# Switched attention: pair matrices on two turned tiles at once, in every second slot, with the routing and rounding steps moved

## The chip, the cores and the metric

One core of one Trainium2 chip. The metric is the device time of one execution of the whole program in microseconds (us). TensorE is called PE, VectorE DVE, ScalarE ACT, GpSimd POOL and SyncE, which issues the DMAs, SP.

## What is computed

A block of four gated layers on x, 128 x 64 x 128 float32, with cross attention and feed forward parts. The change touches only the last part, a switched attention with 8 heads and 8 experts:

```python
logits = jnp.einsum('bsd,ed->bse', x, w)           # w: sel_v_w or sel_o_w
probs = jax.nn.sigmoid(logits.reshape(B, S, H, E))
vals, idx = jax.lax.top_k(probs, K)                # K = 2
vals = vals / jnp.clip(vals.sum(-1, keepdims=True), 1e-09) * route_scale
gate = (jax.nn.one_hot(idx, E) * vals[..., None]).sum(-2)
```

With x normalised per row, q = x q_w, k = x k_w (head size 128), v is the sum over the 8 experts of gate_v times x v_w, the softmax of q k / sqrt(128) over 64 positions multiplies v, and the output is the sum over heads and experts of gate_o times that context times o_w, scaled by a gate and added to the residual. The scores of a head are x (q_w k_w) x, so one 128 x 128 matrix a head, the pair matrix, takes the place of two projections.

## The kernel before

The rows are cut into 64 tiles of 128 (two sequences of 64 positions each). `program` (L2347) runs an opening, a chain of the first layers, and then `switch_attention` (L1731), which is some 60% of the time. There each engine has a list of stages (lag, step), and `straight` (L36) writes the engine's stream out: in slot t every stage in the list's order, each for tile t - lag. Each engine works its stream off in that order; semaphores join the engines. So the work's order is the order of five lists written by hand.

In a slot PE has eight v units, `unit("v", h)`, for the tile of lag 2 and eight o units, `unit("o", h)`, for the tile of lag 3. A unit (L2202 and on) is six matmuls with 512 moving columns in rounded float32 (`F32R`), three each into the banks ps_a and ps_d: high by high, high by low, low by high. `xT_high` is the turned tile rounded, `xT_low` what rounding leaves. ACT's `scale` (L1947) takes ps_a into one of four buffers `scaled`, by the gate, in four activations a unit; DVE's `mix` (L2092) takes ps_d. POOL's `add_v` (L1884) adds both to v (two additions a head), `add_o` does the same for the output, and `finish` (L1922) closes an output tile with three additions. A unit waits for its banks (freed by the unit two before it); ACT's scaling waits for POOL's addition of the unit four before it.

Between the units stand the smaller steps. In PE's list: `turn_x` (L2225) turns the normalised tile into ps_m; `turn_probs` turns the softmax, four heads at a time; `logits` multiplies the turned tile with the routing weights; `pair_keys(0)` and `pair_keys(1)` (L2245) multiply four pair matrices each with one turned tile, into the banks ps_w0 and ps_w1; `scores` (L2271) multiplies the turned tile with uT, what came of the pair matrices; `context` (L2259) multiplies the turned softmax with v, into the same two banks ps_w. A float32 matmul appears as two instructions.

ACT's list has `keep_x` (L1966) after v1: two activations out of ps_m, to xT and to xT_high; `exp_logits` and `keep_probs` after v3; `keep_u(0)` after v5 and `keep_u(1)` after v6 (ps_w to uT); `keep_ctx` and the exponentials among the o units. POOL's list is:

```python
stages = [(2, add_v(0)), (2, add_v(1)), (1, low_x), (4, finish)] + [(2, add_v(h)) for h in range(2, SH)]
stages += [(3, add_o(h)) for h in range(6)] + [(0, rstd)] + [(3, add_o(h)) for h in range(6, SH)]
```

`low_x` (L1877) waits for xT_high of its tile. DVE's list has the mixes and, between them, the 20 routing operations (`route`, L2121), the row maximum, `low_ctx`, the moments of the next tile, and in slots 2 and 3 the splitting of the 16 halves of the o weights (`low_o`, L2060); ACT rounds these halves in the same slots (`round_o`), and SP's list brings them (`fetch_o`, L1859) through four buffers.

Of the kernel before, what the change touches and what calls it, by code (L numbers as in the profile page):

```python
# [1730 lines left out]
def switch_attention(k, A, C, x_in, out):  # L1731
# [6 lines left out]
    with k.scope():  # L1738
# [31 lines left out]
        place = k.sb("sw_place", [P, 2 * SH, SE])  # L1770
# [3 lines left out]
        r = {n: k.sb("sw_r_" + n, G) for n in ("plus", "p", "eq1", "w1", "sel1", "p2", "eq2", "w2", "sel2", "sel")}  # L1774
# [47 lines left out]

        with nc.Block() as block:
            @block.sync
            def _(sp):
# [5 lines left out]
                sp.dma_start(place[:], A["c_place"].rearrange("p (g e) -> p g e", e=SE)).then_inc(q["place"], 16)  # L1831
# [35 lines left out]
                straight([(0, fetch), (1, only_first(fetch_v)), (1, only_first(fetch_o(0, 4))), (2, fetch_residual),  # L1867
                          (2, only_first(fetch_o(4, 10))), (3, only_first(fetch_o(10, 16))), (4, store)])
# [4 lines left out]
            def _(pool):  # L1873
# [65 lines left out]
                stages = [(2, add_v(0)), (2, add_v(1)), (1, low_x), (4, finish)] + [(2, add_v(h)) for h in range(2, SH)]  # L1939
                stages += [(3, add_o(h)) for h in range(6)] + [(0, rstd)] + [(3, add_o(h)) for h in range(6, SH)]  # L1940
# [3 lines left out]
            def _(act):  # L1944
# [90 lines left out]
            def _(dve):  # L2035
# [85 lines left out]
                def route(n):  # L2121


                    def step(i, s, rd):
                        ops = [
                            lambda: dve.tensor_scalar(r["plus"][:], decays[:], 1.0, None, ALU.add),
                            lambda: dve.reciprocal(r["p"][:], r["plus"][:]),
                            lambda: dve.tensor_reduce(rm["m1"][:], r["p"][:], AX.X, ALU.max),
                            lambda: dve.tensor_tensor(r["eq1"][:], r["p"][:], wide(rm["m1"][:]), ALU.is_equal),
                            lambda: dve.tensor_tensor(r["w1"][:], r["eq1"][:], place[:], ALU.mult),  # L2130
                            lambda: dve.tensor_reduce(rm["w1"][:], r["w1"][:], AX.X, ALU.max),
                            lambda: dve.tensor_tensor(r["sel1"][:], r["w1"][:], wide(rm["w1"][:]), ALU.is_equal),
                            lambda: dve.scalar_tensor_tensor(out=r["p2"][:], in0=r["sel1"][:], scalar=-2.0, in1=r["p"][:],
                                                             op0=ALU.mult, op1=ALU.add),
                            lambda: dve.tensor_reduce(rm["m2"][:], r["p2"][:], AX.X, ALU.max),
                            lambda: dve.tensor_tensor(r["eq2"][:], r["p2"][:], wide(rm["m2"][:]), ALU.is_equal),
                            lambda: dve.tensor_tensor(r["w2"][:], r["eq2"][:], place[:], ALU.mult),
                            lambda: dve.tensor_reduce(rm["w2"][:], r["w2"][:], AX.X, ALU.max),
                            lambda: dve.tensor_tensor(r["sel2"][:], r["w2"][:], wide(rm["w2"][:]), ALU.is_equal),
                            lambda: dve.tensor_tensor(r["sel"][:], r["sel1"][:], r["sel2"][:], ALU.add),  # L2140
                            lambda: dve.tensor_tensor(chosen[:, s], r["p"][:], r["sel"][:], ALU.mult),
# [245 lines left out]
```

## Time and profile before

| | before |
|---|---|
| three runs, us | 3166.52, 3166.97, 3173.21 (median 3166.97) |
| the profiled execution, us | 3168.74 |
| its span, first to last instruction, us | 3167.0 |
| busy in the span, us | PE 2907.0, DVE 2780.7, ACT 2341.8, POOL 2322.8 |
| granted TensorE clock, mean | 0.941 of full speed |
| DMA, mean | 17 GB/s |

The span holds all layers. The profiled execution has its own time, 1.8 us above the median of the three runs, and a duration read from the trace belongs to it. Busy is the time in which an engine has an instruction; matmuls overlap, so for PE the start of one to the start of the next is the better measure. An idle time in brackets stands in front of the instruction that ended it, with what released it.

### The profile page before, as it was taken

What the parts mean: (1) busy time and instruction counts of PE and PEld (TensorE: products, weight loads), DVE (VectorE), ACT (ScalarE), POOL (GpSimd) and SP (SyncE); (2) the same over time, 40 slices, a digit from 0 to 9 for tenths busy, and PEclk for the clock granted to TensorE, in tenths of its full rate; (3) what the DMA queues carried; (4) which work ended last, traced back from release to release, by engine and by line L of the source; (5) the groups of instructions that cost most, each with busy time, mean ns of one, the idle gap of its engine ahead of it and who ended that gap; (6) DMA issues with size and microseconds to landing.
All of it is one profiled execution on the core that took longest, in us unless ns stands there. A gap on an engine that the chain in (4) does not pass through costs nothing.

```text
span 3167.0 us, 78218 instructions
## 1 busy us (share of the span) xinstructions
PE 2907.0 (92%) x24620; PEld 2176.0 (69%) x24620; DVE 2780.7 (88%) x9085; ACT 2341.8 (74%) x7546; POOL 2322.8 (73%) x3112
## 2 busy tenths in 40 slices
PE   7489992897689996999999999999999999999998
PEld 7257762675357774677777777777777777777776
DVE  6789997899989986888888888898898898898897
ACT  4866668888976665777777777777777777777776
POOL 2799994666876662677777777777777777777777
PEclk8589995898789997999999999999999999999999
DMA  4000000220000004100000000000000000000000
GB/s 131 8 2 2 2 2 18 68 75 13 1 6 16 16 16 109 30 9 8 7 9 8 7 9 8 7 9 8 7 9 8 8 9 8 7 9 8 7 8 6
DMA packets 114508, 55.31 MB, mean 17 GB/s; under 512 B 18352, under 2 KB 113712, under 8 KB 114096
## 3 DMA queue, kind: packets, MB, share of 16 engines
q1 hardware_dynamic: 114096, 50.30, 5.8%
q8 instruction: 200, 3.28, 0.4%
q14 instruction: 212, 1.74, 0.2%
HBM read 41.81 MB, written 8.45 MB: 16 GB/s over the span
## 4 chain that ended last, share of the span: by engine, by line
PE 59%; DVE 1%; ACT 1%; POOL 1%; DMA 0%; issue 0%; SPq 0%; POOLq 0%; ACTq 0%; DVEq 0%
PE ps_sw_a L2221 24%; PE ps_sw_d L2221 22%; PE ps_sw_w L2267 4%; PE ps_sw_w L2254 3%; PE ps_sw_s L2236 2%; PE ps_sw_s L2278 2%; PE ps_sw_m L2243 1%; ACT sw_scaled L1962 0%; DVE sw_v_part L2117 0%; PE ps_sw_m L2229 0%; DMA sw_v<-in_L_ffn_v_w 0%; POOL sw_v_pair L1889 0%; DVE sw_v_low L2056 0%; DVE sw_o_low L2063 0%; ACT sw_v_high L2017 0%
## 5 line engine op out<-in xcount | busy, mean ns | idle before, releaser
L1962 ACT ACTIVATE sw_scaled<-ps_sw_a,sw_gate_o 128x128 f32<-128x128 f32 x2048 | 620.3, 447 | 254.1 <-PE ps_sw_a L2221 247.0
L1962 ACT ACTIVATE sw_scaled<-ps_sw_a,sw_gate_v 128x128 f32<-128x128 f32 x2048 | 597.3, 448 | 196.2 <-PE ps_sw_a L2221 194.4
L2117 DVE SCALAR_TENSOR_TENSOR sw_o_part<-ps_sw_d,sw_gate_o,sw_o_part 128x128 f32<-128x128 f32 x1920 | 555.6, 339 | 63.1 <-PE ps_sw_d L2221 60.5
L1889 POOL TENSOR_TENSOR sw_v_pair<-sw_v_part,sw_scaled 128x256 f32<-128x256 f32 x512 | 381.9, 746 | 157.0 <-DVE sw_v_part L2117 91.6
L2117 DVE SCALAR_TENSOR_TENSOR sw_v_part<-ps_sw_d,sw_gate_v,sw_scaled 128x128 f32<-128x128 f32 x1024 | 303.9, 337 | 126.1 <-PE ps_sw_d L2221 107.1
L1915 POOL TENSOR_TENSOR sw_o_rest<-sw_o_rest,sw_scaled 128x256 f32<-128x256 f32 x384 | 285.4, 743 | 158.0 <-ACT sw_scaled L1962 120.7
L2117 DVE SCALAR_TENSOR_TENSOR sw_v_part<-ps_sw_d,sw_gate_v,sw_v_part 128x128 f32<-128x128 f32 x1024 | 304.8, 339 | 0.0
L1918 POOL TENSOR_TENSOR sw_o_rest<-sw_o_rest,sw_scaled 128x256 f32<-128x256 f32 x384 | 282.6, 736 | 30.1
L1894 POOL TENSOR_TENSOR sw_v<-sw_v_pair 128x128 f32<-128x128 f32 x512 | 244.6, 478 | 40.1
L1014 POOL TENSOR_TENSOR at_key_wide<-at_keyT,c_half_heads 128x1024 f32<-128x1024 f32 x128 | 242.6, 1895 | 4.6 <-ACT at_keyT L1112 4.6
L2221 PE MATMUL ps_sw_a<-sw_v_high,sw_xT_high 128*128 128x512 f32 x512 | 234.5, 458 | 8.2 <-DVE sw_v_low L2056 8.2
L2221 PE MATMUL ps_sw_a<-sw_o_high,sw_ctx_high 128*128 128x512 f32 x512 | 215.7, 421 | 0.2 <-ACT sw_scaled L1962 0.2
L2221 PE MATMUL ps_sw_d<-sw_v_high,sw_xT_high 128*128 128x512 f32 x512 | 207.6, 405 | 0.3 <-DVE sw_v_part L2117 0.3
L2221 PE MATMUL ps_sw_d<-sw_o_high,sw_ctx_high 128*128 128x512 f32 x512 | 202.1, 395 | 1.2 <-DVE sw_v_part L2117 1.2
L2221 PE MATMUL ps_sw_d<-sw_o_low,sw_ctx_high 128*128 128x512 f32 x512 | 202.7, 396 | 0.0
L2221 PE MATMUL ps_sw_a<-sw_o_high,sw_ctx_low 128*128 128x512 f32 x512 | 202.7, 396 | 0.0
L2221 PE MATMUL ps_sw_a<-sw_v_high,sw_xT_low 128*128 128x512 f32 x512 | 202.5, 396 | 0.0
L2221 PE MATMUL ps_sw_a<-sw_v_low,sw_xT_high 128*128 128x512 f32 x512 | 202.2, 395 | 0.0
L2221 PE MATMUL ps_sw_d<-sw_o_high,sw_ctx_low 128*128 128x512 f32 x512 | 202.1, 395 | 0.0
L2221 PE MATMUL ps_sw_a<-sw_o_low,sw_ctx_high 128*128 128x512 f32 x512 | 202.1, 395 | 0.0
L2221 PE MATMUL ps_sw_d<-sw_v_high,sw_xT_low 128*128 128x512 f32 x512 | 201.8, 394 | 0.0
L2221 PE MATMUL ps_sw_d<-sw_v_low,sw_xT_high 128*128 128x512 f32 x512 | 200.7, 392 | 0.0
(337 smaller groups left out, 8511.3 us busy)
## 6 DMA issues: line engine op xcount, KB each, us to landing
re_values<-in_ctx SPq DMA_DIRECT2D x128, 64.0 KB, 2.4
l_ctx<-in_ctx SPq DMA_DIRECT2D x16, 256.0 KB, 4.5
x<-in_x SPq DMA_DIRECT2D x16, 256.0 KB, 4.6
re_ctx<-in_ctx SPq DMA_DIRECT2D x16, 256.0 KB, 3.1
scratch_x<-x SPq DMA_DIRECT2D x64, 64.0 KB, 1.5
sw_x<-scratch_x SPq DMA_DIRECT2D x64, 64.0 KB, 1.9
sw_x_res<-scratch_x SPq DMA_DIRECT2D x64, 64.0 KB, 1.8
out<-sw_y SPq DMA_DIRECT2D x64, 64.0 KB, 1.5
```

What stands on the lines that cost most here:

```text
L1014: pool.tensor_tensor(key_wide[:, s], keyT[:, s].unsqueeze(1).broadcast_to([P, HALF, P]), C["half_heads"][:].unsqueeze(2).broadcast_to([P, ...
L1889: pool.tensor_tensor(v_pair[:, h % 2], v_part[:, h], scaled[:, h % 4, 2:4], ALU.add)\
L1894: pool.tensor_tensor(v[:, h], v_pair[:, h % 2, 0], v_pair[:, h % 2, 1], ALU.add).then_inc(q["v"], 1)
L1915: pool.tensor_tensor(o_rest[:, 0:2], o_rest[:, 0:2], scaled[:, h % 4, 0:2], ALU.add)\
L1918: pool.tensor_tensor(o_rest[:, 2:4], o_rest[:, 2:4], scaled[:, h % 4, 2:4], ALU.add)\
L1962: act.activation(scaled[:, h % 4, e], ps_a[h % 2][:, e], ACT.Copy, scale=gates[:, s, h, HALF_E + e:HALF_E + e + 1]).then_inc(a_scaled[kind ...
L2117: dve.scalar_tensor_tensor(out=acc[:, e % 2], in0=ps_d[h % 2][:, e], scalar=gates[:, s, h, e:e + 1], in1=before, op0=ALU.mult, op1=ALU.add ...
L2221: m = pe.matmul(bank, lhs[a], w[b][:, h, experts], start=c == 0, stop=c == 2)
L2236: m = pe.matmul(ps_s[t, h], probs[t, s, h], C["ident"][t, t], start=True, stop=True)
L2254: m = pe.matmul(ps_w[n][:, h * P:(h + 1) * P], W["pair"][:, 4 * n + h], xT[:, s], start=True, stop=True)
L2267: m = pe.matmul(ps_w[b][:, h * S:(h + 1) * S], v[t, h], probs_T[t, h], start=True, stop=True)
L2278: m = pe.matmul(ps_s[t], xT[:, s, t], uT[:, :, t], start=True, stop=True)
```

## The change

The lags of nearly everything behind the turning of a tile grow by two: logits, routing, scores and exponentials from 1 to 3, v units from 2 to 4, o units from 3 to 5, finish from 4 to 6. xT has four buffers instead of two and uT holds two tiles. The pair matrices are multiplied for an even tile and the one after it at once, so with 256 moving columns, in every second slot: two groups of 4 matmuls, one behind the first four turned heads of the softmax, one behind v4. keep_x keeps xT alone; the rounding to xT_high is the new step round_x, of lag 3. The routing's ten buffers become three, written in place, and place is one row broadcast. The splitting of the o weights keeps its lags, 2 and 3.

```diff
-        xT = k.sb("sw_xT", [P, 2, P])
+        xT = k.sb("sw_xT", [P, 4, P])
-        uT = k.sb("sw_uT", [P, SH, P])
+        uT = k.sb("sw_uT", [P, SH, 2, P])
...
-        place = k.sb("sw_place", [P, 2 * SH, SE])
+        place = k.sb("sw_place", [P, SE])
-        r = {n: k.sb("sw_r_" + n, G) for n in ("plus", "p", "eq1", "w1", "sel1", "p2", "eq2", "w2", "sel2", "sel")}
+        r = {n: k.sb("sw_r_" + n, G) for n in ("equal", "sel", "p2")}
...
+        def of_pair(step):
+            def at(i, s, rd):
+                if i % 2 == 0:
+                    step(i, s, rd)
+            return at
...
-                straight([(0, fetch), (1, only_first(fetch_v)), (1, only_first(fetch_o(0, 4))), (2, fetch_residual),
-                          (2, only_first(fetch_o(4, 10))), (3, only_first(fetch_o(10, 16))), (4, store)])
+                straight([(0, fetch), (1, only_first(fetch_v)), (1, only_first(fetch_o(0, 4))), (4, fetch_residual),
+                          (2, only_first(fetch_o(4, 10))), (3, only_first(fetch_o(10, 16))), (6, store)])
...
-                stages = [(2, add_v(0)), (2, add_v(1)), (1, low_x), (4, finish)] + [(2, add_v(h)) for h in range(2, SH)]
-                stages += [(3, add_o(h)) for h in range(6)] + [(0, rstd)] + [(3, add_o(h)) for h in range(6, SH)]
+                stages = [(4, add_v(0)), (4, add_v(1)), (3, low_x), (6, finish)] + [(4, add_v(h)) for h in range(2, SH)]
+                stages += [(5, add_o(h)) for h in range(6)] + [(0, rstd)] + [(5, add_o(h)) for h in range(6, SH)]
...
                 def keep_x(i, s, rd):
                     act.wait_ge(q["x_turned"], i + 1)
+                    if not first(i, 4):
+                        act.wait_ge(q["scores"], i - 3)
+                        act.wait_ge(q["xT_low"], i - 3)
+                    act.activation(xT[:, i % 4], ps_m[:, 0], ACT.Copy).then_inc(q["xT"], 1)
+
+                def round_x(i, s, rd):
+                    act.wait_ge(q["xT"], i + 1)
                     if not first(i, 2):
-                        act.wait_ge(q["scores"], i - 1)
                         act.wait_ge(q["xT_low"], i - 1)
                         act.wait_ge(d_made["v"], SH * (i - 1))
-                    act.activation(xT[:, s], ps_m[:, 0], ACT.Copy).then_inc(q["xT"], 1)
-                    act.activation(xT_high[:, s], ps_m[:, 0], ACT.Copy).then_inc(q["xT_high"], 1)
+                    act.activation(xT_high[:, s], xT[:, i % 4], ACT.Copy).then_inc(q["xT_high"], 1)
...
-                stages = vs[:2] + [(1, keep_x)] + vs[2:4] + [(1, exp_logits), (2, keep_probs)] + vs[4:6]
-                stages += [(1, keep_u(0)), vs[6], (1, keep_u(1)), vs[7]] + os[:3] + [(2, keep_ctx(0)), os[3], exps[0]]
-                stages += [os[4], (2, keep_ctx(1)), os[5], exps[1], os[6], exps[2], os[7], exps[3]]
+                stages = vs[:2] + [(1, keep_x), vs[2], (3, keep_u(0)), vs[3], (3, keep_u(1)), (3, exp_logits), (4, keep_probs)]
+                stages += [vs[4], (3, round_x), vs[5], (3, keep_u(2)), vs[6], (3, keep_u(3)), vs[7]] + os[:3]
+                stages += [(4, keep_ctx(0)), os[3], exps[0], os[4], (4, keep_ctx(1)), os[5], exps[1], os[6], exps[2], os[7], exps[3]]
...
-                def pair_keys(n):
+                def pair_keys(lo):
                     def step(i, s, rd):
...
+                        if lo == 0:
+                            pe.wait_ge(q["xT"], i + 2)
+                        for n in (lo, lo + 1):
+                            if n >= 2:
+                                pe.wait_ge(q["uT"], 2 * i + n - 1)
+                            elif i == 0:
+                                pe.wait_ge(prep["kept"], 3)
+                            else:
+                                pe.wait_ge(q["ctx_low"], 2 * (i - 2) + n + 1)
+                            both = xT[:, i % 4:i % 4 + 2].rearrange("p c t -> p (c t)")
+                            for h in range(2):
+                                m = pe.matmul(ps_w[n % 2][:, 2 * h * P:2 * (h + 1) * P], W["pair"][:, 2 * n + h], both,
+                                              start=True, stop=True)
+                            m.then_inc(q["u"], 1)
+                    return of_pair(step)
...
-                stages = vs[:2] + [(1, turn_x), turns[0], vs[2], turns[1], (1, logits), vs[3], vs[4], (1, pair_keys(0))]
-                stages += [vs[5], (1, pair_keys(1)), vs[6], vs[7], os[0], (1, scores), os[1], (2, context)]
-                stages += os[2:]
+                stages = vs[:2] + [(1, turn_x), turns[0], (3, pair_keys(0)), vs[2], turns[1], (3, logits), vs[3], vs[4], (3, pair_keys(2))]
+                stages += vs[5:] + [os[0], (3, scores), os[1], (4, context)] + os[2:]
```

ACT's keep_u has four parts now (0 to 3) that run in the same slots as the pair groups, each after the unit named in the list. DVE's list keeps its order with the new lags.

## Rows read from the trace of the kernel before

**Rows 1.** Windows of two neighbouring slots: busy us and instructions of each engine.
```profile
2406.70:2436.30 29.60, 29.60 (x184) 22.68 (x184) 26.56 (x96) 22.55 (x91) 22.64 (x36) 1.00 0.03 9
2436.30:2465.90 29.60, 29.60 (x184) 22.69 (x183) 26.59 (x96) 22.54 (x91) 22.64 (x36) 1.00 0.03 8
```

**Rows 2.** Timeline of PE in one slot: start, duration, line, operation, count.
```profile
2406.72 0.47 PE L2221 MATMUL ps_sw_a<-sw_v_high,sw_xT_high 128*128 128x512 f32 x1
...
2410.56 0.50 PE L2221 MATMUL ps_sw_a<-sw_v_high,sw_xT_high 128*128 128x512 f32 x1
...
2413.00 0.47 PE L2221 MATMUL ps_sw_a<-sw_v_high,sw_xT_high 128*128 128x512 f32 x1
...
2414.47 0.39 PE L2221 MATMUL ps_sw_a<-sw_v_high,sw_xT_high 128*128 128x512 f32 x1
...
2415.61 0.39 PE L2221 MATMUL ps_sw_d<-sw_v_high,sw_xT_low 128*128 128x512 f32 x1
2415.83 1.05 PE L2254 MATMUL ps_sw_w<-sw_xT,sw_pair 128*128 128x128 f32 x8
2416.64 0.48 PE L2221 MATMUL ps_sw_a<-sw_v_high,sw_xT_high 128*128 128x512 f32 x1
2416.95 0.40 PE L2221 MATMUL ps_sw_a<-sw_v_low,sw_xT_high 128*128 128x512 f32 x1
...
2425.50 0.40 PE L2221 MATMUL ps_sw_d<-sw_o_high,sw_ctx_low 128*128 128x512 f32 x1
2425.83 2.00 PE L2267 MATMUL ps_sw_w<-sw_probs_T,sw_v 64*128 64x64 f32 x32
```

**Rows 3.** Timeline of ACT in the same slot.
```profile
2410.42 0.61 ACT L1972 ACTIVATE sw_xT<-ps_sw_m 128x128 f32<-128x128 f32 x1
2410.57 0.61 ACT L1973 ACTIVATE sw_xT_high<-ps_sw_m 128x128 fp32r<-128x128 f32 x1
...
2413.97 1.14 ACT L1962 ACTIVATE sw_scaled<-ps_sw_a,sw_gate_v 128x128 f32<-128x128 f32 x4 [1.27 <-PE ps_sw_a L2221]
...
2415.62 1.18 ACT L1962 ACTIVATE sw_scaled<-ps_sw_a,sw_gate_v 128x128 f32<-128x128 f32 x4
...
2419.89 1.14 ACT L1962 ACTIVATE sw_scaled<-ps_sw_a,sw_gate_v 128x128 f32<-128x128 f32 x4 [0.64 <-PE ps_sw_a L2221]
2420.90 0.61 ACT L1993 ACTIVATE sw_uT<-ps_sw_w 128x512 f32<-128x512 f32 x1
2421.38 1.16 ACT L1962 ACTIVATE sw_scaled<-ps_sw_a,sw_gate_v 128x128 f32<-128x128 f32 x4
```

**Rows 4.** Timeline of POOL in the same slot.
```profile
2413.31 0.46 POOL L1881 TENSOR_TENSOR sw_xT_low<-sw_xT,sw_xT_high 128x128 fp32r<-128x128 f32 x1
2413.73 0.73 POOL L1925 TENSOR_TENSOR sw_o_pair<-sw_o_rest 128x256 f32<-128x256 f32 x1
...
2415.82 0.72 POOL L1889 TENSOR_TENSOR sw_v_pair<-sw_v_part,sw_scaled 128x256 f32<-128x256 f32 x1
...
2417.04 0.74 POOL L1889 TENSOR_TENSOR sw_v_pair<-sw_v_part,sw_scaled 128x256 f32<-128x256 f32 x1
...
2419.86 0.74 POOL L1889 TENSOR_TENSOR sw_v_pair<-sw_v_part,sw_scaled 128x256 f32<-128x256 f32 x1 [0.27 <-DVE sw_v_part L2117]
...
2422.13 0.74 POOL L1889 TENSOR_TENSOR sw_v_pair<-sw_v_part,sw_scaled 128x256 f32<-128x256 f32 x1 [1.00 <-ACT sw_scaled L1962]
...
2424.40 0.74 POOL L1889 TENSOR_TENSOR sw_v_pair<-sw_v_part,sw_scaled 128x256 f32<-128x256 f32 x1 [1.00 <-DVE sw_v_part L2117]
2425.22 0.46 POOL L1894 TENSOR_TENSOR sw_v<-sw_v_pair 128x128 f32<-128x128 f32 x1
```

**Rows 5.** Timeline of ACT, then of DVE, at the stage's beginning.
```profile
1225.77 0.27 ACT L1973 ACTIVATE sw_xT_high<-ps_sw_m 128x128 fp32r<-128x128 f32 x1
...
1250.67 0.61 DVE L2117 SCALAR_TENSOR_TENSOR sw_v_part<-ps_sw_d,sw_gate_v,sw_scaled 128x128 f32<-128x128 f32 x2 [0.64 <-issue]
...
1251.71 0.68 DVE L2063 TENSOR_TENSOR sw_o_low<-sw_o_part,sw_o_high 128x512 fp32r<-128x512 f32 x1
...
1270.18 0.68 DVE L2063 TENSOR_TENSOR sw_o_low<-sw_spare,sw_o_high 128x512 fp32r<-128x512 f32 x1
...
1279.99 0.61 DVE L2117 SCALAR_TENSOR_TENSOR sw_v_part<-ps_sw_d,sw_gate_v,sw_scaled 128x128 f32<-128x128 f32 x2 [1.11 <-ACT sw_scaled L1962]
```

More of the change, by code:

```diff
@@ L1830, in _ @@
                 sp.dma_start(route_scale[:], on_all(A["L3_ffn_route_scale"], 1)).then_inc(prep["small"], 16)
[L1831 removed]
+                sp.dma_start(place[:], A["c_place"][:, 0:SE]).then_inc(q["place"], 16)
                 def tile_in(dst, i):
@@ L1880, in low_x @@
                         pool.wait_ge(d_made["v"], SH * (i - 1))
-                    pool.tensor_tensor(xT_low[:, s], xT[:, s], xT_high[:, s].bitcast(F32), ALU.subtract)\
+                    pool.tensor_tensor(xT_low[:, s], xT[:, i % 4], xT_high[:, s].bitcast(F32), ALU.subtract)\
                         .then_inc(q["xT_low"], 1)
@@ L1990, in step @@
                         act.wait_ge(q["u"], 2 * i + n + 1)
-                        if n == 0 and not first(i, 1):
+                        if n == 0 and i:
                             act.wait_ge(q["scores"], i)
-                        act.activation(uT[:, 4 * n:4 * n + 4], ps_w[n].rearrange("p (h t) -> p h t", h=4), ACT.Copy)\
-                            .then_inc(q["uT"], 1)
-                    return step
+                        act.activation(uT[:, 2 * n:2 * n + 2], ps_w[n % 2].rearrange("p (h c t) -> p h c t", h=2, c=2),
+                                       ACT.Copy).then_inc(q["uT"], 1)
+                    return of_pair(step)
                 def keep_ctx(b):
@@ L2124, in step @@
                     def step(i, s, rd):
+                        p = decays
                         ops = [
[L2126 to L2130, printed above, removed]
@@ new lines, in step @@
+                            lambda: dve.tensor_tensor(r["equal"][:], p[:], wide(rm["m1"][:]), ALU.is_equal),
+                            lambda: dve.tensor_tensor(r["equal"][:], r["equal"][:], place[:].unsqueeze(1).broadcast_to(G), ALU.mult),
+                            lambda: dve.tensor_reduce(rm["w1"][:], r["equal"][:], AX.X, ALU.max),
+                            lambda: dve.tensor_tensor(r["sel"][:], r["equal"][:], wide(rm["w1"][:]), ALU.is_equal),
+                            lambda: dve.scalar_tensor_tensor(out=r["p2"][:], in0=r["sel"][:], scalar=-2.0, in1=p[:],
@@ L2140, in step @@
-                            lambda: dve.tensor_tensor(r["sel"][:], r["sel1"][:], r["sel2"][:], ALU.add),
-                            lambda: dve.tensor_tensor(chosen[:, s], r["p"][:], r["sel"][:], ALU.mult),
+                            lambda: dve.tensor_tensor(r["equal"][:], r["p2"][:], wide(rm["m2"][:]), ALU.is_equal),
+                            lambda: dve.tensor_tensor(r["equal"][:], r["equal"][:], place[:].unsqueeze(1).broadcast_to(G), ALU.mult),
+                            lambda: dve.tensor_reduce(rm["w2"][:], r["equal"][:], AX.X, ALU.max),
@@ L2226, in turn_x @@
                     pe.wait_ge(q["xhat"], i + 1)
-                    if not first(i, 1):
-                        pe.wait_ge(q["decays"], i)
+                    if i >= 1:
+                        pe.wait_ge(q["xT"], i)
+                    if i >= 3:
+                        pe.wait_ge(q["decays"], i - 2)
                     pe.transpose(ps_m[:, 0], L["xhat"][:, s], C["ident"][:]).then_inc(q["x_turned"], 1)
@@ L2241, in logits @@
                         pe.wait_ge(prep["kept"], 1)
-                    pe.wait_ge(q["xT_high"], i + 1)
-                    pe.matmul(ps_m[:, 1], xT[:, s], W["sel"][:], start=True, stop=True).then_inc(q["logits"], 1)
-                def pair_keys(n):
+                    pe.wait_ge(q["xT"], min(i + 3, TILES))
+                    pe.matmul(ps_m[:, 1], xT[:, i % 4], W["sel"][:], start=True, stop=True).then_inc(q["logits"], 1)
+                def pair_keys(lo):
                     def step(i, s, rd):
-                        if i == 0:
-                            pe.wait_ge(prep["kept"], 2 + n)
-                        elif not first(i, 2):
-                            pe.wait_ge(q["ctx_low"], 2 * (i - 2) + n + 1)
-                        else:
-                            pe.wait_ge(q["uT"], 1 + n)
-                        for h in range(4):
-                            m = pe.matmul(ps_w[n][:, h * P:(h + 1) * P], W["pair"][:, 4 * n + h], xT[:, s],
-                                          start=True, stop=True)
-                        m.then_inc(q["u"], 1)
-                    return step
+                        if lo == 0:
[12 more added lines that the diff above has]
+                            m.then_inc(q["u"], 1)
+                    return of_pair(step)
@@ L2271, in scores @@
                 def scores(i, s, rd):
-                    waits = [(q["uT"], 2 * i + 2)]
+                    waits = [(q["uT"], 4 * (i // 2) + 4)]
                     if not first(i, 1):
@@ L2277, in scores @@
                         t = slice(b * S, (b + 1) * S)
-                        m = pe.matmul(ps_s[t], xT[:, s, t], uT[:, :, t], start=True, stop=True)
+                        m = pe.matmul(ps_s[t], xT[:, i % 4, t], uT[:, :, s, t], start=True, stop=True)
                     m.then_inc(q["scores"], 1)
```

42 lines of the change are left out of this document (22 added, 20 removed).

## The prediction

> **What bounds the kernel now.** I read the page's busy shares first, then the windows of two neighbouring slots of the switched stage, then one such slot engine by engine in the timeline. A slot is one turn of the order written out in the code: eight v units, eight o units, and everything placed between them. In the two windows PE is busy 29.60 of 29.60 us at full clock, DVE 26.56, POOL 22.64 and ACT 22.55 [rows 1]; 64 tiles at 29.6 us are 1894 of the 3167 us. So PE sets the time there, and the question is whether anything makes it wait. All offsets below count from the first v matmul of the slot, 2406.72 [rows 2].
>
> PE's order in a slot: v2 begins at 3.84, v3 at 6.28, v4 at 7.75, a pair group of 8 instructions at 9.11, and the context at 19.11. The last o matmul before the context begins at 2425.50; at the plain pitch of 0.23 (five in 1.14, 2414.47 to 2415.61) the context could begin at 2425.73, and it begins at 2425.83 [rows 2]. What it waits for is POOL's eighth v, 2425.22 + 0.46 = 2425.68 [rows 4], plus a handover of 0.15. **The context has only 0.1 us of slack against POOL.** POOL itself, between the xT_low subtraction at 6.59 and that last v, stands idle 0.27, 1.00 and 1.00, together 2.27 us [rows 4]. ACT is late only at the slot's start: it rounds xT_high at 3.85, scales v3 at 7.25 after 1.27 us of idleness, and v4 at 8.90 [rows 3]. POOL takes xT_low with no wait, because xT_high has lain ready for 2.5 us.
>
> **The change, part by part.** (1) The pair matmuls. Now a tile has two groups of 8 instructions of 128 columns. From the matmul before a group to the second one after it takes 2415.61 to 2416.95, 1.34 us, against 0.46 for two plain pitches: a group costs 0.89 [rows 2], four of them, two tiles, 3.56. Afterwards two tiles have 16 instructions of 256 columns, all in the odd slot. 0.89 over 8 is 0.111 for 128 columns, or 0.107 without the joints; at 0.2133 for 256 columns the 16 cost 3.41, with two joints of 0.04 left 3.49. That saves 0.07 per two tiles, 2 us in the run. The bounds: nothing at all, and 1.78 per two tiles if an instruction of 256 columns cost no more than one of 128, 57 us. The first is nearer: columns rule PE's rows, since 512 single-pass columns take 0.23 there. The Trainium skill ("TensorE: Matmul & The Clock Gate", Back-to-back issue gap) gives a sustained 81 ns a matmul at 128 columns and 131 at 512, which would put it near the second bound; the pitch of 0.23 at 512 columns here contradicts it.
>
> (2) Placement. In odd slots pair(0), 8 x 0.2133 = 1.71 us, stands ahead of v2; pair(2), 1.71 again, after v4. In even slots both are gone, and PE could be at the context 1.78 us sooner.
>
> (3) The rounding. This is the costly one. keep_x was one step with both activations, at 3.70 and 3.85. Now only xT is kept there, and round_x, which makes xT_high, stands in ACT's order **behind the scaling of v4**, at the same lag (3) as POOL's low_x. So POOL's wait on xT_high becomes a wait within the slot, and low_x is still POOL's third step: behind it are queued finish (three additions) and add_v(2) to add_v(7), on which the context hangs, and ACT's scaling too, whose buffers come free by these additions.
> Even slot: ACT's v4 begins at 8.90, four scalings take 1.01 (2419.89 to 2420.90) [rows 3], so round_x begins at 9.91; 0.27 for it alone [rows 5] and 0.15 handover put low_x at 10.3 instead of 6.59, 3.7 later. From there POOL goes without a gap: 0.42, 2.09 for finish, six additions of v at 1.23 (2415.82 to 2417.04) [rows 4]. Of the 3.7 its old idleness takes up 2.27 and the context's slack 0.1: **the context comes 1.3 later**. The 1.78 that PE gains on the way is lost in that wait.
> Odd slot: pair(0) puts v2, v3 and v4 on PE off by 1.71. keep_u(0) fits into ACT's old idleness of 1.27 before v3, but keep_u(1), 0.48 (2420.90 to 2421.38) [rows 3], stands between v3 and v4. ACT's v4 is 2.2 later, and low_x 3.7 + 2.2 = 5.9. Less 2.37: **the context comes 3.5 later**, of which pair(0) and pair(2) alone would have asked 1.6 beyond the old slot. After the context each slot goes on as now (ACT, DVE and POOL all wait for PE there), so a shift of the context is a longer slot.
> Sixty-one slots have low_x, finish and the v units together (6 to 66), 31 even and 30 odd: 31 x 1.3 + 30 x 3.5 = 145 us; slot 5, without finish, some 2.
>
> (4) Two more slots of lead. v units start in slot 4 instead of 2, but the splitting of the o weights stays in slots 2 and 3. DVE now does the first split at 1251.71 between the first mixes, and mixes tile 1 from 1279.99; the last split of slot 2 is at 1270.18 [rows 5]. Afterwards all 16 splits stand ahead of the first mix. Without mixes between them they are paced by their DMAs and by rounding; I estimate 20 to 25 us for both slots, so tile 0's mixes begin near 1272 instead of 1250.67. Given back: the slots that follow have no splits, 16 x 0.6, and the next tiles' softmax is ready. I take +9, between 0 and +20. The last slots are as now.
>
> (5) At nothing: ten routing buffers become three and place is broadcast, but the 20 operations are the same, and DVE has 3.0 us idle in a slot [rows 1]; without that cover each 0.1 us more per operation would be 2 us a tile. In odd slots the first routing step waits some 0.8 for the later exp, and DVE is shifted with PE. The residual load and the store are moved by two slots on SP's queue with their readers; the place load shrinks outside the loop.
>
> Sum: 145 + 2 + 9 = 156 us. Against the profiled execution (3167.0 span, 3168.74 in all) it is 3325; the three runs' median, 3166.97, lies 1.8 below, so I say 3323.
>
> **Rivals.** *A smaller loss* (0.07): POOL's chain gives way somewhere, or 256 columns are cheap, so that pair(0) shifts ACT's v4 by 0.85 less: 25 us off, and with half of the even slots' loss 45 off. 3210 to 3280. *A larger one* (0.03): scaling of v6 and v7 waits for the late add_v(2) and add_v(3), PE's units o0 and o1 for their banks, and this goes on past the context; one more us a slot gives 3385. *The change does nothing* (0.05): the wait on xT_high is hidden, and 2 us of saving stand against 9 of lead: 3174, from 3160 to 3185. It would need xT_high in 2.37 us after the old low_x, before 8.96, while ACT begins v4 only at 8.90 and round_x stands behind it. *Faster* (0.03): the same hidden wait and 256 columns at the price of 128, 0.89 a tile: 3167 - 57 + 9 = 3119. It decides once the rounding is visible before 8.96 and the wide group takes under 1.2 us instead of 1.71. The first speaks against the code's order, the second against the 0.23 of a 512-column matmul. By the page's two figures the time would be near this rival's, and its 0.03 is what these rows leave of it.
>
> **How the numbers follow.** The likeliest case (0.82) spans 3285 to 3365: 0.3 us either way on the shifts is 20, the lead another 10. To hold 8 in 10 and take in part of the smaller loss the range is 3255 to 3365. About 0.2% (6 us) is what a measurement here can tell from none. Faster: 0.03 and a little of the hidden case, 0.04. Same: 0.03. Slower: 0.93.
>
> **What would show it.** PE no longer full in the switched stage, with waits for POOL's v before the context of about 1.3 us in odd and 1.4 in even slots; POOL idle about 3.7 (even) and 5.9 (odd) before low_x, released by ACT's rounding; contexts alternating by about 31 and 33 us instead of 29.6; the wide group at 1.71 for 8 instructions; ACT waiting for POOL before scaling v6 in even slots, and o0 on PE some 1.5 us behind it. I am wrong if POOL waits little before low_x, if the context follows its o unit at 0.33, or if the slot keeps 29.6. If slots are as forecast but the end is not, the lead was mis-sized.

## The result, and the profile after

| | before | after |
|---|---|---|
| median beside each other on one chip, us | 3167.64 (4 runs) | 3359.66 (4 runs) |
| lowest and highest, us | 3166.52 to 3173.21 | 3349.52 to 3364.54 |
| the profiled execution, us | 3168.74 | 3358.62 |
| its span, us | 3167.0 | 3356.8 |
| granted TensorE clock, mean | 0.941 | 0.937 |

The changed kernel is slower: ratio 1.0598, 95% interval 1.0571 to 1.0626. The forecast was 3323 (3255 to 3365); between the two profiled executions the change costs 189.9 us, where the sum said 156.

The page of the changed kernel: span and busy times, the chain that ended last, and one of the costly groups (busy and mean ns, then the idle time before it and who ended it).

```profile
span 3356.8 us, 77191 instructions
...
PE 2972.7 (89%) x24108; PEld 2160.3 (64%) x24108; DVE 2797.1 (83%) x9085; ACT 2352.1 (70%) x7546; POOL 2322.8 (69%) x3112
...
POOL 26%; PE 19%; issue 12%; ACT 3%; DVE 3%; POOLq 0%; DMA 0%; SPq 0%; ACTq 0%; DVEq 0%
...
L1887 POOL TENSOR_TENSOR sw_xT_low<-sw_xT,sw_xT_high 128x128 fp32r<-128x128 f32 x64 | 29.6, 462 | 315.2 <-ACT sw_xT_high L1984 315.2
```

POOL's 64 subtractions for xT_low last 30 us together, and POOL stands 315 us idle in front of them, all of it for ACT's rounding. The chain that ended last now runs through POOL more than through PE.

Windows from one context to the next, an even slot and then an odd one (busy us and instructions of PE, PEld, DVE, ACT, POOL, then the granted clock):

```profile
2422.60:2453.66 31.06, 28.97 (x167) 20.59 (x167) 26.52 (x96) 21.73 (x86) 22.73 (x36) 1.00 0.03 8
2453.66:2487.06 33.40, 31.77 (x183) 23.76 (x184) 27.23 (x96) 23.63 (x90) 22.71 (x36) 1.00 0.03 7
```

In [rows 1] PE was busy for all of 29.60; here it misses 2.1 and 1.6 us a slot, at full clock. Some waits between 1400 and 3200 us (us in total, times, longest):

```profile
POOL sw_xT_low L1887 <- ACT sw_xT_high L1984: 274.8, 56, 6.1
...
ACT sw_scaled L1968 <- POOL sw_v_pair L1895: 127.5, 111, 2.6
...
PE ps_sw_w L2288 <- POOL sw_v L1900: 59.6, 55, 1.3
PE ps_sw_a L2233 <- ACT sw_scaled L1968: 37.1, 56, 1.2
```

PE's timeline: the o0 of the even slot, the two contexts that enclose the odd one (their counterpart is the last line of [rows 2]), and between them both wide groups:

```profile
2448.15 0.47 PE L2233 MATMUL ps_sw_a<-sw_o_high,sw_ctx_high 128*128 128x512 f32 x1 [0.98 <-ACT sw_scaled L1968]
...
2453.66 2.00 PE L2288 MATMUL ps_sw_w<-sw_probs_T,sw_v 64*128 64x64 f32 x32 [0.91 <-POOL sw_v L1900]
...
2468.03 1.99 PE L2272 MATMUL ps_sw_w<-sw_xT,sw_pair 128*128 128x256 f32 x8
2469.67 0.58 PE L2233 MATMUL ps_sw_a<-sw_v_high,sw_xT_high 128*128 128x512 f32 x1
...
2474.80 0.39 PE L2233 MATMUL ps_sw_d<-sw_v_high,sw_xT_low 128*128 128x512 f32 x1
2475.03 1.89 PE L2272 MATMUL ps_sw_w<-sw_xT,sw_pair 128*128 128x256 f32 x8
2476.56 0.58 PE L2233 MATMUL ps_sw_a<-sw_v_high,sw_xT_high 128*128 128x512 f32 x1
2476.98 0.40 PE L2233 MATMUL ps_sw_a<-sw_v_low,sw_xT_high 128*128 128x512 f32 x1
...
2487.06 2.00 PE L2288 MATMUL ps_sw_w<-sw_probs_T,sw_v 64*128 64x64 f32 x32 [1.25 <-POOL sw_v L1900]
```

ACT's timeline, the scaling of v6 and v7 in the even slot:

```profile
2446.81 2.36 ACT L1968 ACTIVATE sw_scaled<-ps_sw_a,sw_gate_v 128x128 f32<-128x128 f32 x8 [2.33 <-POOL sw_v_pair L1895]
```

POOL's timeline (compare [rows 4]), with the subtraction in an even and in an odd slot:

```profile
2443.51 0.46 POOL L1887 TENSOR_TENSOR sw_xT_low<-sw_xT,sw_xT_high 128x128 fp32r<-128x128 f32 x1 [3.75 <-ACT sw_xT_high L1984]
2443.93 0.74 POOL L1931 TENSOR_TENSOR sw_o_pair<-sw_o_rest 128x256 f32<-128x256 f32 x1
...
2453.16 0.45 POOL L1900 TENSOR_TENSOR sw_v<-sw_v_pair 128x128 f32<-128x128 f32 x1
...
2476.76 0.46 POOL L1887 TENSOR_TENSOR sw_xT_low<-sw_xT,sw_xT_high 128x128 fp32r<-128x128 f32 x1 [6.11 <-ACT sw_xT_high L1984]
```

From 2443.51 to 2453.16 POOL has no bracket: it works without a gap from the late rounding to v's last addition, and the context starts right behind that. Gone are the three idle times of [rows 4].

**Where the 189.8 us of span went.** The starts of the 64 contexts divide the stage. The first is at 1287.76 instead of 1272.22, 15.5 later; the last at 3323.39 instead of 3133.60, and behind it both kernels take 33.4. So the slots between cost 174.3. Against the usual 29.61, thirty odd slots are 33.40 long (114 us more), twenty even ones 31.04 (29 us), ten even ones 32.44 (28 us), one 34.19 (4.6 us); the mean before was a little over the usual one, which takes 1 us off this sum. The eleven long even slots owe their extra length to PE's clock, which the last section shows.

### The profile page after: what moved, and what is told of

Its sections match the earlier page's. It is cut to its first block, busy times and chain, and to the rows that moved or that the text cites. A ratio compares the mean times of both kernels' runs of the same rounds, so it can differ in the third digit from the quotient of the medians.

```text
span 3356.8 us, 77191 instructions
## 1 busy us (share of the span) xinstructions
PE 2972.7 (89%) x24108; PEld 2160.3 (64%) x24108; DVE 2797.1 (83%) x9085; ACT 2352.1 (70%) x7546; POOL 2322.8 (69%) x3112
## 4 chain that ended last, share of the span: by engine, by line
POOL 26%; PE 19%; issue 12%; ACT 3%; DVE 3%; POOLq 0%; DMA 0%; SPq 0%; ACTq 0%; DVEq 0%
PE ps_sw_a L2233 7%; POOL sw_v_pair L1895 7%; POOL sw_o_rest L1921 6%; POOL sw_o_rest L1924 6%; PE ps_sw_d L2233 5%; POOL sw_v L1900 4%; PE ps_sw_w L2288 4%; ACT sw_scaled L1968 3%; DVE sw_v_part L2128 1%; POOL sw_o_pair L1933 1%; POOL sw_o_pair L1931 1%; PE ps_sw_w L2272 1%; PE ps_sw_s L2299 1%; POOL sw_y L1937 1%; POOL sw_xT_low L1887 1%
## 5 line engine op out<-in xcount | busy, mean ns | idle before, releaser
L2233 PE MATMUL ps_sw_a<-sw_o_high,sw_ctx_high 128*128 128x512 f32 x512 | 224.4, 438 | 40.9 <-ACT sw_scaled L1968 40.9
L1887 POOL TENSOR_TENSOR sw_xT_low<-sw_xT,sw_xT_high 128x128 fp32r<-128x128 f32 x64 | 29.6, 462 | 315.2 <-ACT sw_xT_high L1984 315.2
L2233 PE MATMUL ps_sw_d<-sw_o_high,sw_ctx_high 128*128 128x512 f32 x512 | 211.7, 414 | 5.4 <-DVE sw_v_part L2128 5.3
```

What stands on the lines that cost most here:

```text
L1887: pool.tensor_tensor(xT_low[:, s], xT[:, i % 4], xT_high[:, s].bitcast(F32), ALU.subtract)\
L2233: m = pe.matmul(bank, lhs[a], w[b][:, h, experts], start=c == 0, stop=c == 2)
```

## The experiments

The kernels ran on several chips, whose medians of the kernel before lie between 3166.22 and 3173.60. So the table gives each kernel's ratio to the kernel before on the same chip (95% interval), and what one trace says of the contexts (the slots are the usual ones of the middle of the stage). A difference of a few us between traces of two chips can be the chips'. Four kernels, e7, e9, e10 and e12, leave out most of the routing; they only show what DVE's work costs.

| kernel | median, us | ratio, 95% interval | first context | odd, even slot |
|---|---|---|---|---|
| changed kernel | 3359.66 | 1.0571 to 1.0626 | 1287.76 | 33.40, 31.04 |
| e1 rounding early | 3257.35 | 1.0245 to 1.0280 | 1287.89 | 32.18, 29.55 |
| e2 before, rounding late | 3274.05 | 1.0306 to 1.0336 | 1271.52 | 31.06, 31.06 |
| e3 xT_low late on POOL | 3250.04 | 1.0234 to 1.0264 | 1283.20 | 32.18, 29.44 |
| e4 splits with the v units | 3354.26 | 1.0557 to 1.0589 | 1273.15 | 33.39, 31.04 |
| e5 e1 without the pairing | 3175.22 | 1.0017 to 1.0036 | 1283.82 | 29.63, 29.63 |
| e6 e1 and e4 | 3250.75 | 1.0244 to 1.0287 | 1273.83 | 32.17, 29.55 |
| e7 e1, some routing short | 3228.96 | 1.0178 to 1.0223 | 1280.35 | 31.79, 29.24 |
| e8 e1, 128 columns | 3251.19 | 1.0253 to 1.0287 | 1286.04 | 32.20, 29.53 |
| e9 e1, routing bare | 3180.28 | 1.0016 to 1.0034 | 1282.08 | 31.28, 28.15 |
| e10 before, routing bare | 3163.65 | 0.9967 to 0.9985 | 1269.70 | 29.64, 29.64 |
| e11 e5 and e4 | 3171.34 | 0.9997 to 1.0014 | 1273.88 | 29.63, 29.63 |
| e12 changed, routing bare | 3333.69 | 1.0500 to 1.0558 | 1281.14 | 33.10, 30.86 |

### e1: the rounding back behind keep_x

```diff
-stages = vs[:2] + [(1, keep_x), vs[2], (3, keep_u(0)), ...
+stages = vs[:2] + [(1, keep_x), (3, round_x), vs[2], (3, keep_u(0)), ...
-stages += [vs[4], (3, round_x), vs[5], ...
+stages += [vs[4], vs[5], ...
```

> The changed kernel with round_x moved directly behind keep_x, where the rounding stood before; all else as changed. Theory 1 (POOL's wait before low_x is the loss): the wait is gone, the odd slot is bound by PE at 29.60 + 1.64 = 31.2 us, the even slot at 27.9, and with the lead of 15.5 read from the changed kernel's first context the time is 3167 + 15.5 - 2 = 3180, within 8. Rival (the wide groups' place ahead of v2 holds up ACT and DVE by itself): the odd slots stay over 32.5 and the time is 3200 to 3290. Rival (lags and buffers): nothing changes, 3357.

Measured 3257.35, 84 above before and not the 3180 of the theory. The time is in the first rival's band, but the odd slots are not over its 32.5; the span is 100 below the changed kernel's. The waits on xT_high are gone from the trace, yet a slot is still 1.26 longer than before on average (32.18 and 29.55). The late rounding is about half of the loss; the other half I had not seen.

### e2: the late rounding alone, in the kernel before

```diff
-                    act.activation(xT_high[:, s], ps_m[:, 0], ACT.Copy).then_inc(q["xT_high"], 1)
+                def round_x(i, s, rd):
+                    act.wait_ge(q["xT"], i + 1)
+                    act.activation(xT_high[:, s], xT[:, s], ACT.Copy).then_inc(q["xT_high"], 1)
...
-[(1, exp_logits), (2, keep_probs)] + vs[4:6]
+[(1, exp_logits), (2, keep_probs), vs[4], (1, round_x), vs[5]]
...
-pe.wait_ge(q["xT_high"], i + 1)
+pe.wait_ge(q["xT"], i + 1)
```

(The last pair is the wait of `logits`, which reads xT and need not wait for the rounding.)

> The kernel before with one part of the change: the rounding is a step of its own behind the scaling of v4, at the old lag, and reads xT. Theory 1: POOL stands idle 3.7 us before low_x in every slot and the context comes 1.4 us later, 31.0 instead of 29.60: 3167 + 61 x 1.43 = 3254, or up to 3290 if the waits let TensorE's clock fall in some slots as in the changed kernel. Rival (the loss is in the wide groups or the lags): 3167, at most 3175.

Measured 3274.05, and slots of 31.06. POOL's and PE's timelines of e2, the subtraction and the context of one slot:

```profile
2418.96 0.46 POOL L1881 TENSOR_TENSOR sw_xT_low<-sw_xT,sw_xT_high 128x128 fp32r<-128x128 f32 x1 [3.88 <-ACT sw_xT_high L1976]
```
```profile
2429.15 2.00 PE L2270 MATMUL ps_sw_w<-sw_probs_T,sw_v 64*128 64x64 f32 x32 [0.89 <-POOL sw_v L1894]
```

One moved activation, 0.38 us in its new place, makes every slot 1.45 longer, and to the same 31.0 as the even slots of the changed kernel, though PE has a different amount of work in the two. Eleven of e2's slots are longer still (32.4 to 32.9), by the clock.

### e3: xT_low behind the additions of v

```diff
-stages = [(4, add_v(0)), (4, add_v(1)), (3, low_x), (6, finish)] + [(4, add_v(h)) for h in range(2, SH)]
+stages = [(4, add_v(0)), (4, add_v(1)), (6, finish)] + [(4, add_v(h)) for h in range(2, SH)] + [(3, low_x)]
```

> The changed kernel with low_x moved in POOL's order behind add_v(7); round_x stays behind v4. Theory 1 (what costs is what is queued behind the waiting low_x, not the late rounding itself): 3180 within 8, as with the early rounding. Rival (the late rounding costs through another reader, the v units of the next slot): above 3220.

Measured 3250.04, with the slots of e1, while the rounding stays behind v4. The expectation's 3180 was missed as in e1, and the time stands above its rival's 3220, but in its trace PE waits for DVE alone between 1320 and 3150 us, as in e1: what remains is e1's other half. So xT_high is not needed early: it is enough that nothing urgent is queued behind the step that waits for it. The lateness cost nothing; the queue behind it cost all that e1 gives back.

### e4: the splitting of the o weights moved along with the units

The fetches of halves 4 to 15, `round_o` and `low_o` get the lags 4 and 5 for 2 and 3.

```diff
-stages += [(2, low_o(n // 2)), (3, low_o(SH + n // 2))]
+stages += [(4, low_o(n // 2)), (5, low_o(SH + n // 2))]
```

> The changed kernel with the rounding and splitting of the o weights and their DMAs moved to slots 4 and 5, so that they stand between the v units again, as before. If the lead's cost is that all 16 splits stand ahead of the first v unit, the first context comes near 1274 instead of 1287.8 and the time falls by 13 to 16 from the changed kernel's 3360. If it is the two extra slots by themselves, it falls by under 5.

The first context came at 1273.15, 14.6 earlier, as the first branch had it (near 1274). The span fell by only 4, as the second had it: the slot behind the first context is 1.6 longer (29.49), and there are more long slots than in the changed kernel (34.17 twice, and two pairs as 32.96 and 35.16). With the rounding early (e6, below) 11 of the 14 arrive at the end of the span.

### e5: e1 without the pairing

Lags, four xT buffers, three routing buffers, broadcast place and early rounding stay. Each slot has two groups of four 128-column matmuls again, behind v4 and v5, ACT's keep_u has two parts again, and uT holds one tile.

```diff
-both = xT[:, i % 4:i % 4 + 2].rearrange("p c t -> p (c t)")
-for h in range(2):
-    m = pe.matmul(ps_w[n % 2][:, 2 * h * P:2 * (h + 1) * P], W["pair"][:, 2 * n + h], both, start=True, stop=True)
+for h in range(4):
+    m = pe.matmul(ps_w[n][:, h * P:(h + 1) * P], W["pair"][:, 4 * n + h], xT[:, i % 4], start=True, stop=True)
```

> The kernel of e1 (rounding early) with the pairing alone undone: 8 matmuls of 128 columns a tile, in every slot, after v4 and after v5 as before; lags, four xT buffers and the routing as changed. Theory 2 (with POOL's wait gone the rest of the loss is that two tiles' pair matmuls stand in one slot and DVE does not let the other slot shrink): all slots near 29.6, 3167 + 15 = 3182, within 8. Rival (the rest comes from the lags, the buffers or the routing written in place): 3240 to 3260 as in e1.

Measured 3175.22 and slots of 29.63: everything but the pairing (with its place and its four keep_u) is free per slot, and 8 of the 9 us that are left come from the start: the first context is 11.6 later than before, and the slot behind it 3.6 shorter (24.06 against 27.69). The pairing is the second half of the loss, 80 us (the span of e1, 3256.4, less that of e5, 3176.3).

### e6: early rounding and moved splits together

> The kernel of e1 with the splitting of the o weights back between the v units as in e4. If the parts add, the first context comes near 1272.5 instead of 1287.9 and the time is 3257 - 15 = 3242. If the lead is hidden in another wait, 3250 or more.

Measured 3250.75, in the branch of "3250 or more", and its ratio to before is e1's (1.0265 and 1.0263). The traces differ: the span is 11.0 below e1's and the first context 14.1 earlier, at 1273.83, with the slot behind it 2.9 longer. The two ran on different chips, so that the 11 reach the time is not shown. The slots are e1's.

### e7: part of the routing shortened, with the wide groups

```diff
-dve.reciprocal(p[:], p[:])
+dve.reciprocal(p[:, 0:2], p[:, 0:2])
-dve.tensor_tensor(r["sel"][:], r["equal"][:], wide(rm["w1"][:]), ALU.is_equal)
+dve.tensor_tensor(r["sel"][:, 0:2], r["equal"][:, 0:2], wide(rm["w1"][:])[:, 0:2], ALU.is_equal)
```

(and the second such comparison likewise).

> The kernel of e1 with three of the routing's DVE operations (the reciprocal and two comparisons) done on 2 of 16 groups, so some 2 us a slot less on DVE between v3 and o0; this leaves out most of the routing. Theory 2 (DVE holds the even slot at 29.55 and adds 0.9 in the odd one): even slots go to 28.0 to 28.6, odd ones to 31.2 to 31.6, the time to 3180 to 3205. Rival (POOL's or ACT's chain holds them): within 10 of 3257.

Measured 3228.96, between the band of theory 2 (3180 to 3205) and the rival's (within 10 of 3257). The edit took less from DVE than the 2 us expected: its busy time over the run fell by 41.7 (2784.4 to 2742.7, 0.65 a tile). The reciprocal went from 0.94 to 0.24 us, but each of the two comparisons only from 0.80 to 0.68, for an eighth of the elements. The slots fell by 0.39 and 0.31, both kinds nearly alike. DVE counts, by about half of what is taken from it.

### e8: the width alone

Each 256-column matmul of e1 as two of 128 columns, in the same places.

> The kernel of e1 with each matmul of 256 columns made as two of 128 in the same place, same work on all else. By columns alone (2 passes of 128 at 0.107) the group takes the same 1.7 us: 3257, within 5. If width is worth what the first forecast took, 0.07 per two tiles, 3259. If a 128-column matmul is bound by its weight load, over 3270.

Measured 3251.19, a ratio of 1.0270 beside e1's 1.0263, with e1's slots: no loss from narrow matmuls. PE's timeline of e8, the second group:

```profile
2412.86 0.39 PE L2233 MATMUL ps_sw_d<-sw_v_high,sw_xT_low 128*128 128x512 f32 x1
2413.09 1.95 PE L2272 MATMUL ps_sw_w<-sw_xT,sw_pair 128*128 128x128 f32 x16
2414.79 0.48 PE L2233 MATMUL ps_sw_a<-sw_v_high,sw_xT_high 128*128 128x512 f32 x1
2415.11 0.40 PE L2233 MATMUL ps_sw_a<-sw_v_low,sw_xT_high 128*128 128x512 f32 x1
```

From the matmul before the group to the second one after it: 2.25 with 16 narrow ones, 2.18 with 8 wide ones (2474.80 to 2476.98 above). Width is worth 0.07 a group, and nothing to the slot.

### e9 and e10: DVE nearly without routing, with and without the change

All array operations of `route` work on 2 of the 16 groups, in e1 (e9) and in the kernel before (e10).

```diff
-dve.tensor_tensor(r["equal"][:], p[:], wide(rm["m1"][:]), ALU.is_equal)
+dve.tensor_tensor(r["equal"][:, 0:2], p[:, 0:2], wide(rm["m1"][:])[:, 0:2], ALU.is_equal)
```

(and so on through the list).

> e1 (rounding early, pairing kept) with all array operations of the routing on 2 of its 16 groups; it leaves out most of the choice of experts and its gates. e7 took about 0.65 us of VectorE off a tile and the slots became 0.35 us shorter; this takes roughly 1 to 1.5 us more. Theory DVE (in slots with uneven PE work the mixes and the routing between them hold the d banks, and PE waits for them): contexts about 31.4 in odd and 28.6 in even slots, waits of PE for sw_v_part nearly gone, 3185 to 3210. Theory handover (the loss is latency between engines at the wide groups and does not depend on DVE's load): as e7, 3225 to 3232, even slots 29.2.

> The kernel before with the same shortened routing; it leaves out the same part. Control for e9: in even slots of 29.6 us PE is full and DVE has 3 us to spare, so theory DVE expects 29.6 a slot and 3160 to 3168; if the routing also paces PE here the slots fall below 29.4 and the time below 3153, and e9 has to be read against that.

e9 took 3180.28, below its band, its span 77 us below e1's. e10 took 3163.65, its slots are 29.64, and the 4 us that its span is shorter lie around the first context. So with a light DVE nearly the whole price of the pairing is gone (from the first to the last context e9 takes 1864.0 us and e10 1859.9), and before the change DVE's routing is free in every slot. First e1: an even slot as a window, PE in the unit o0, and DVE's timeline ahead of it:

```profile
2487.60:2517.14 29.54, 28.70 (x167) 20.66 (x167) 26.59 (x96) 21.70 (x88) 22.71 (x35) 1.00 0.03 8
```
```profile
2512.46 0.39 PE L2233 MATMUL ps_sw_a<-sw_o_high,sw_ctx_low 128*128 128x512 f32 x1
2513.45 0.50 PE L2233 MATMUL ps_sw_d<-sw_o_high,sw_ctx_high 128*128 128x512 f32 x1 [0.60 <-DVE sw_v_part L2128]
```
```profile
2508.23 0.51 DVE L2128 SCALAR_TENSOR_TENSOR sw_v_part<-ps_sw_d,sw_gate_v,sw_scaled 128x128 f32<-128x128 f32 x2
...
2509.79 0.60 DVE L2128 SCALAR_TENSOR_TENSOR sw_v_part<-ps_sw_d,sw_gate_v,sw_scaled 128x128 f32<-128x128 f32 x2
...
2511.36 0.80 DVE L2144 TENSOR_TENSOR sw_r_sel<-sw_r_equal,sw_m_w 128x128 f32<-128x128 f32 x1
2512.09 0.60 DVE L2128 SCALAR_TENSOR_TENSOR sw_v_part<-ps_sw_d,sw_gate_v,sw_scaled 128x128 f32<-128x128 f32 x2
...
2514.36 0.59 DVE L2128 SCALAR_TENSOR_TENSOR sw_v_part<-ps_sw_d,sw_gate_v,sw_scaled 128x128 f32<-128x128 f32 x2
```

The units of PE would be 1.37 apart there (six pitches of 0.23); the first mixes of v4 to v7 on DVE are 1.56, 2.30 and 2.27 apart, as the routing stands between them. The two d banks are held, and the second half of o0 starts 0.99 behind the last matmul of the first instead of 0.23. DVE's timeline of the kernel before has the same pace:

```profile
2416.84 0.51 DVE L2117 SCALAR_TENSOR_TENSOR sw_v_part<-ps_sw_d,sw_gate_v,sw_scaled 128x128 f32<-128x128 f32 x2
...
2418.39 0.60 DVE L2117 SCALAR_TENSOR_TENSOR sw_v_part<-ps_sw_d,sw_gate_v,sw_scaled 128x128 f32<-128x128 f32 x2
...
2420.67 0.60 DVE L2117 SCALAR_TENSOR_TENSOR sw_v_part<-ps_sw_d,sw_gate_v,sw_scaled 128x128 f32<-128x128 f32 x2
...
2422.94 0.60 DVE L2117 SCALAR_TENSOR_TENSOR sw_v_part<-ps_sw_d,sw_gate_v,sw_scaled 128x128 f32<-128x128 f32 x2
```

But there a pair group of 0.89 stood in this stretch twice in every slot, and DVE kept up under it. An even slot has none now, and DVE sets the pace; an odd slot has 1.7 in it, and as much ahead of v2, where DVE only waits for PE (2.30 us at 2473.23). Now e9, an odd and an even slot:

```profile
2406.38:2437.66 31.28, 31.28 (x184) 23.96 (x183) 24.37 (x95) 23.45 (x92) 22.63 (x35) 1.00 0.03 8
2437.66:2465.82 28.16, 28.10 (x168) 20.85 (x167) 23.79 (x95) 21.69 (x88) 22.61 (x35) 1.00 0.03 8
```

PE is full again. The waits of PE for DVE between 1400 and 3200 us, first in e1, then in e9:

```profile
PE ps_sw_d L2233 <- DVE sw_v_part L2128: 32.3, 65, 0.6
```
```profile
PE ps_sw_d L2237 <- DVE sw_v_part L2132: 0.4, 2, 0.2
```

Two slots now take 59.44, before 59.22 (e10: 59.28): even with DVE out of the way the pairing does not win.

### e11: the best of the changed kernel

e5 with the splits of e4.

> e5 (after without the pairing, rounding early) with the splitting of the o weights put back between the v units. e5 took 3175 with its first context 11.6 us later than before; e4 and e6 showed 10 to 14 us earlier. If lead and pairing are all that is left: 3162 to 3167, within 0.2% of before (no version with the wide groups can beat it). If the two more slots of lead cost something beyond the splitting: 3170 to 3176.

Measured 3171.34 beside 3171.98: no difference. In absolute time that lies in the second branch (3170 to 3176), but the bands were set from another chip's 3166, and the ratio is what counts; the first context is 1.7 behind before. With the pairing, the rounding and the splits undone, what is left of the change costs nothing and brings nothing. No kernel that computes everything was faster than the one before.

### e12: does the second loss add to the first?

The routing of e9 in the changed kernel as it is.

> The changed kernel as it is (rounding behind v4) with the shortened routing of e9; it leaves out the same part. With the rounding early, this took 77 us off (e1 to e9). Theory chain (as the changed kernel stands, POOL's chain behind the late rounding sets the slot, and VectorE's load lies beside it, so the two losses overlap instead of adding up): contexts still 31.0 in even and 33.0 to 33.4 in odd slots, 3335 to 3360. Theory sum (the two losses stand one behind the other): 77 off here too, 3275 to 3290.

Windows of e12, an odd slot and an even one, and its wait for the rounding:

```profile
2435.93:2469.02 33.09, 31.82 (x184) 23.79 (x183) 25.74 (x98) 24.08 (x93) 22.54 (x36) 1.00 0.03 7
2469.02:2499.90 30.88, 28.69 (x168) 20.69 (x168) 25.58 (x96) 21.69 (x86) 22.52 (x36) 1.00 0.03 7
```
```profile
POOL sw_xT_low L1887 <- ACT sw_xT_high L1984: 273.2, 56, 6.6
```

Measured 3333.69, just under the band of theory chain and far from theory sum's. Its span is 25 below the changed kernel's, 6.6 of it in the first context; from e1 to e9 it was 77. The slots hardly moved, 33.40 to 33.10 and 31.04 to 30.86, and the wait for the rounding stayed. In the changed kernel POOL's chain sets the slot, and DVE's lateness lies mostly beside it. So the pairing has about one price by two routes. From the first context to the last, which leaves the lead out, it costs 67 us with the rounding late (2035.6 less e2's 1968.5), by POOL's chain and in the odd slots alone: 33.40 against 31.06, while the even ones are equal. With the rounding early it costs 76 (e1's 1935.1 less e5's 1859.1), by DVE, and in both kinds of slot it misses what PE alone would take.

## Why the prediction was right, and where it was not

**The rounding (3): right, mechanism and size.** low_x was to come 3.7 and 5.9 later, and POOL's idle time before it is 3.75 and 6.11. (By [rows 3] xT_high had lain ready for 2.13 us before, 2413.31 less 2411.18, and not 2.5; no term hangs on it.) The context was to come 1.3 and 3.5 later; that gives slots of 30.9 and 33.1, and e12, in which DVE is out of the way, has 30.86 and 33.10. The changed kernel itself has 31.04 and 33.40: the 0.15 and 0.3 more are DVE's, some 14 us. ACT's wait for POOL before v6 (2.33), the later o0 (0.98 of waiting) and PE's wait before the context are all there. That last one was forecast as 1.4 in even slots and 1.3 in odd ones; it is 0.91 and 1.25, and in the even slot a part of the loss stands ahead of o0 instead. e2 and e3 show the same thing from both sides: the step moved alone makes the loss, and nothing queued behind it unmakes it.

**The wide groups (1) and their place (2): right in size.** Group 2.18 less two pitches is 1.72, two tiles 3.44 against 3.56: 0.12 saved, forecast 0.07. That even slots let PE come 1.78 sooner was too much even for PE alone: e9's 28.15 is 1.46 shorter than before (its 31.28 is 1.67 longer, forecast 1.6). In e1, at 29.55, DVE leaves next to nothing of it.

**The operations at nothing (5): this step failed, hidden behind (3).** I took DVE's 3.0 us idle in a slot as cover for the routing, and put its effect at nothing. The 3.0 is an average of a slot; in the stretch from v4 to o0, with its routing, DVE is slower than PE's units, and what covered it was PE's own pair groups, which the change takes out of every second slot. What the runs show in its place is 76 us where the rounding is early (e1 less e5, nearly all gone in e9), and some 14 us in the changed kernel (e12). Had the rounding been hidden, I would have said 3174, the rival that the change does nothing. e1 is that case, and it takes 3257. The rival's chance was small, but its price was 83 us too low.

**The lead (4): +15.5 instead of +9.** The mixes of tile 0 began at 1270.64, as estimated (near 1272), 20 later than [rows 5]. Of the "16 x 0.6" given back 4.5 came: from first mix to first context 21.55 before and 17.12 after. The other eight splits gave nothing: the slot that had them before (27.69 to the second context) is no longer than the same slot without them (27.89).

**Left out: the clock, 17 us.** Ten even slots lose 1.4 each and one 3.15. No term stood for it.

The difference of forecast and result is then: 6.5 in the lead, 17 by the clock, 9 in 30 odd slots (0.3 each) and 4 in the even ones, less the 2 for slot 5. That is 34.5, and the sum was short by 34. What I missed had one sign, and the range held by 5 us; neither the clock nor DVE was in its bounds. That the time lies inside is in part luck: the main term was sound, the edge was not.

## What to carry to other kernels

Moving one short step in an in-order queue costs whatever is queued behind the step that waits for it: read the consumer's list past its wait, and if the value isn't urgent, move the consumer too (e3). An engine that is 90% busy (DVE, 26.56 of 29.60 us) is not covered by its average idle time: work bunched on another engine, even at the same sum, takes the cover from one stretch and puts it in another where it is of no use. And behind the bound that a change makes, a second one may stand at nearly the same price: read the waits again after each undoing, before the first answer is believed.

## What the runs showed of the hardware

**Half clock behind a wait.** In ten of the eleven long even slots PE's clock falls for some 3.5 us after the context, in the one of 34.19 for twice as long. Windows of such a slot, then its beginning in steps of 2 us, and two PE rows, the context and a matmul behind it:

```profile
1380.09:1412.53 32.44, 30.37 (x167) 21.84 (x167) 26.79 (x96) 21.79 (x86) 22.61 (x36) 0.95 0.02 7
...
1378.00:1380.00 2.00, 0.82 (x4) 0.35 (x2) 1.97 (x7) 1.14 (x4) 1.84 (x5) 1.00 0.11 33
1380.00:1382.00 2.00, 1.91 (x32) 1.86 (x32) 1.97 (x8) 0.00 (x0) 1.49 (x3) 1.00 0.00 0
1382.00:1384.00 2.00, 2.00 (x7) 1.60 (x6) 0.12 (x1) 0.50 (x2) 0.00 (x0) 0.57 0.00 0
1384.00:1386.00 2.00, 2.00 (x7) 1.54 (x7) 1.22 (x6) 1.17 (x5) 1.20 (x2) 0.58 0.00 0
1386.00:1388.00 2.00, 2.00 (x10) 1.63 (x9) 1.50 (x7) 2.00 (x10) 1.03 (x2) 1.00 0.00 0
```
```profile
1380.09 2.00 PE L2288 MATMUL ps_sw_w<-sw_probs_T,sw_v 64*128 64x64 f32 x32 [1.26 <-POOL sw_v L1900]
...
1382.84 0.63 PE L2233 MATMUL ps_sw_a<-sw_o_high,sw_ctx_low 128*128 128x512 f32 x1
```

Ahead of the fall PE waited 1.26 us for POOL's v. From 1382.0 to 1385.8 its matmuls are 0.43 apart instead of 0.23, the lower level of 1.2 GHz, and the slot is 1.4 longer. The same wait, 1.25 at 2487.06, stands ahead of slots without a fall, so what decides isn't shown. Such a wait can thus cost again what it lasted. The kernels with PE waits before the context (changed kernel, e2, e4, and e12, where they last up to 0.8) have such long slots; behind the second context e1, whose longest PE wait in the stage is 0.6, has none, nor have e3 and e5 to e11. The Trainium skill ("TensorE: Matmul & The Clock Gate", "Wait — 56ns, not 53.3ns?") puts matmuls of 512 columns 426.7 ns apart in the low state, and the 0.43 agrees.

**Width.** The second groups of e8 and of the changed kernel give 1.70 us for 16 matmuls of 128 columns, 0.106 each, and 1.53 for 8 of 256 columns, 0.191 each; in rounded float32, 512 columns take 0.23. From 128 to 256 columns the cost in float32 goes nearly by the columns. Joining two tiles saves 0.17 between the group's own starts, but the matmul behind the wide group comes later, and 0.07 a group is left, as e8 shows.
